# Adding the causal mask of a 16-head attention by VectorE in PSUM instead of by products on TensorE

## The chip, the cores and the metric

The kernel runs on one core of one Trainium2 chip. The metric is the device time of one execution in microseconds. The engines are TensorE (PE, with its weight loads shown as PEld), VectorE (DVE), ScalarE (ACT), GpSimd (POOL) and SyncE (SP), each with a queue of its own that it works through in order; they wait for one another on semaphores.

## The reference

The whole network has four layers of gated cross-attention and feed-forward on x of shape (4, 512, 128). The change lies in the feed-forward of the third layer, whose first half is a causal self-attention with 16 heads of width 64, run here for four batch elements of 512 tokens:

```python
ckv = x @ Wkva
kv_latent, k_rope = (ckv[:, :, :R], ckv[:, :, R:])
...
q = jnp.concatenate([q_nope, _rope(q_rope)], axis=-1)
k = jnp.concatenate([kv, _rope(k_rope)], axis=-1)
v = jnp.concatenate([kv, jnp.zeros_like(k_rope)], axis=-1)
att = jnp.einsum('bhqd,bhkd->bhqk', q, k) / jnp.sqrt(jnp.float32(D))
mask = jnp.tril(jnp.ones((t, t), dtype=bool))
att = jnp.where(mask, att, jnp.float32(-jnp.inf))
att = jax.nn.softmax(att, axis=-1)
y = jnp.einsum('bhqk,bhkd->bhqd', att, v)
```

The mixture of experts behind it, and the other layers, are not touched.

## The kernel before

The program is a sequence of blocks. `attention_2f(k, b, ...)` is the block of this attention, called once for each of the four batch elements. In it each engine has its own stream (`block.tensor`, `block.scalar`, `block.vector`, `block.gpsimd`). First come a normalisation and the projections with the rotation; then a loop over 32 units.

A unit u is one pair of heads (two of 16, side by side in the array's rows 0 to 63 and 64 to 127) and one tile of 128 queries. The four tiles of a pair come in the order 0, 1, 3, 2 (`tile_of`), and since attention is causal, tile t needs only the first 128(t+1) keys (`keys`): so the units of a pair have 128, 256, 512 and 384 keys. Here a unit is called by that number of keys; a pair (of heads) is four units. The last 128 keys of each unit are the diagonal tile, where the mask is needed: `causal` holds 0 on and below the diagonal and -3e38 above it.

What each engine does in one step of the loop, in its own order:

- PE (lines 2110 to 2122): `scores(u)`, lines 2058 to 2074, which needs the score banks that unit u-2 used, so it waits until both exps of u-2 are done (`s.ex`). It makes the products of both heads in two halves of the keys, then adds the mask to the diagonal tile by one product per head of a bf16 unit matrix with `causal_h`, a bf16 copy of `causal`, and signals `s.s`. Every eighth step `values(g)`, lines 2088 to 2099, the products with the latents for four heads. Then `turn(u-3, 0)` and `turn(u-3, 1)`, lines 2076 to 2086: transposes of the normalised rows of the two heads; each waits for POOL's normalised row (`s.pn`) and for the copy of the unit before out of its bank (`s.ca`, `s.cb`).
- DVE (lines 2203 to 2216): `copy_second(u-4)`, line 2201; `row_max(u)`, lines 2187 to 2191, the negated maximum of each head's row, read from PSUM; `reciprocals(u-1)`, line 2195.
- ACT (lines 2157 to 2172): `copy_first(u-3)`, line 2150; `exps(u)`, line 2142, one for each head, with the row's sum.
- POOL: `normalise(u)`, line 2026, each head's row times its reciprocal.

The score banks are four PSUM banks: two heads by two units in turn. After the loop come the last transposes, output products and the residual. The setup block makes `causal_h` once (line 589).

Of the kernel before, what the change touches and what calls it, by code (L numbers as in the profile page):

```python
# [16 lines left out]
BF16 = mybir.dt.bfloat16  # L17
I32 = mybir.dt.int32
ALU = mybir.AluOpType
# [3 lines left out]
P = 128  # L23
# [45 lines left out]
def flamingo_kernel(nc, a, at, early_at, out):  # L69
    with ExitStack() as ctx:  # L70
# [22 lines left out]
        def sb(name, shape, dt=FP32):  # L93
            return ctx.enter_context(nc.sbuf_tensor(name, shape, dt))
# [3 lines left out]
        def bank(i, n=1):  # L98
            return psum[:, 512 * i:512 * (i + n)]
# [40 lines left out]
        ident, causal, fold32 = resident("ident", P), resident("causal", P), resident("fold32", 32)  # L140
# [73 lines left out]
        qtt = part(region_b, 0, [P, PAIRS, S])  # L214
        turned_f = part(region_a, 0, [P, 4, T, S])
        krot = part(region_a, 4 * T * S, [P, S])
# [74 lines left out]
        latv = sb("latv", [P, T, 2 * LAT])  # L291
# [114 lines left out]
                       gsum=sb("gsum_f", [P, T]))  # L406
        back_ws = [set_m, back_w2, back_w3]
        ident_h = sb("ident_h", [P, P], BF16)
        causal_h = sb("causal_h", [P, P], BF16)
        fold_h = sb("fold_h", [96, 32], BF16)  # L410

        def over(ap, axis, shape):
            return ap.unsqueeze(axis).broadcast_to(shape)
# [85 lines left out]
        def setup(s):  # L499
# [77 lines left out]
            def vector(dve):  # L577
                link = chained(dve, s.dve)
                half = HD3 // 2
                yield 0  # L580
                nc.vector.memset(mka[:, :, :], 0.0)
                nc.vector.memset(latv[:, :, :], 0.0)
                nc.vector.memset(kctx[:, :, :], 0.0)
                nc.vector.memset(mkb[:, :, :], 0.0)
                nc.vector.memset(mqb[:, :, :], 0.0)
                nc.vector.memset(mqa[:, :, :], 0.0).then_inc(s.cleared, 1)
                dve.wait_ge(s.front_in, all_front)
                nc.vector.tensor_copy(ident_h[:, :], ident[:, :])
                nc.vector.tensor_copy(causal_h[:, :], causal[:, :])
                nc.vector.tensor_copy(fold_h[:, :], fold32[:, :])  # L590
                link(nc.vector.tensor_scalar(scale3[:, :], rs3[:, :], 1.0, None, ALU.add))
                yield 3
                for h in range(H3):
                    nc.vector.tensor_scalar(wk3a[:, h, :], wkv3[:, 0, :], scale3[:, 0:1], None, ALU.mult)
                    nc.vector.tensor_scalar(wk3b[:, h, 0:half], wkv3[:, 0, half:], scale3[:, 0:1], -1.0, ALU.mult, ALU.mult)
                    nc.vector.tensor_scalar(wk3b[:, h, half:], wkv3[:, 0, 0:half], scale3[:, 0:1], None, ALU.mult)
                    mm = nc.vector.tensor_scalar(wv3[:, h, :], wkv3[:, 1, :], scale3[:, 0:1], None, ALU.mult)
                mm.then_inc(s.wk3, 1)
                yield 7
                dve.wait_ge(s.exp2, 1)  # L600
                for _ in fp4_quantise(link, fw0[:, :, :], exp2_w[:, :], (big_r, big_r2), red[:, 0:4], red2[:, 0:4]):
                    pass
                nc.vector.tensor_tensor(big_r, big_r, over(red2[:, 0:4], 2, [P, 4, 32]), ALU.mult).then_inc(s.quantised, 1)
                yield 8
                nc.vector.tensor_scalar(wq3b[:, :, 0:half], wq3[:, :, half:], scale3[:, 0:1], -1.0, ALU.mult, ALU.mult)
                link(nc.vector.tensor_scalar(wq3b[:, :, half:], wq3[:, :, 0:half], scale3[:, 0:1], None, ALU.mult))
                link(nc.vector.tensor_scalar(wq3[:, :, :], wq3[:, :, :], scale3[:, 0:1], None, ALU.mult))
                yield 17
                dve.wait_ge(s.rest_in, all_rest)
                for r in range(2):  # L610
                    nc.vector.tensor_scalar(mka[:, r, 0:32], mkva[:, LAT:LAT + ROPE], wl1[:, 0:1], None, ALU.mult)
                    nc.vector.tensor_scalar(mka[:, r, 32:48], mkva[:, 0:LAT], wl1[:, 0:1], None, ALU.mult)
                    turn_k = mkb[:, r, 0:32].rearrange("p (i two) -> p i two", two=2)
                    pair_k = mkva[:, LAT:LAT + ROPE].rearrange("p (i two) -> p i two", two=2)
                    nc.vector.tensor_scalar(turn_k[:, :, 0], pair_k[:, :, 1], wl1[:, 0:1], -1.0, ALU.mult, ALU.mult)
                    nc.vector.tensor_scalar(turn_k[:, :, 1], pair_k[:, :, 0], wl1[:, 0:1], None, ALU.mult)
                dve.wait_ge(s.early_in, 16)
                dve.wait_ge(s.wl1_scaled, 1)
                nc.vector.tensor_scalar(mqa[:, :, 0:32], mq2[:, :, 32:64], rtmp[:, 0:1], None, ALU.mult)
                turn_q = mqb[:, :, 0:32].rearrange("p h (i two) -> p h i two", two=2)  # L620
                pair_q = mq2[:, :, 32:64].rearrange("p h (i two) -> p h i two", two=2)
                nc.vector.tensor_scalar(turn_q[:, :, :, 0], pair_q[:, :, :, 1], rtmp[:, 0:1], -1.0, ALU.mult, ALU.mult)
                nc.vector.tensor_scalar(turn_q[:, :, :, 1], pair_q[:, :, :, 0], rtmp[:, 0:1], None, ALU.mult)
                yield 21
                dve.wait_ge(s.be1_w2, E8)
                nc.vector.tensor_tensor(bias2[:, :], psum[:, 4 * 512:6 * 512], b2, ALU.add)
                for pair in range(4):
                    yield 22 + pair
                    dve.wait_ge(s.w2_mean, 1)
                    for e in (2 * pair, 2 * pair + 1):  # L630
                        cols = w2[:, FC * e:FC * (e + 1), 0:D]
                        mean = bank(6 + e // 4)[:, 128 * (e % 4):128 * (e % 4) + 128]
                        nc.vector.tensor_tensor(cols, cols, over(mean, 1, [P, FC, D]), ALU.subtract)
# [24 lines left out]
        NORM = ("stat", "mv", "rstd", "xn", "xt", "xnt")  # L658
# [923 lines left out]
        def attention_2(k, b, combined=None, last=None, also_load=None):  # L1582
# [75 lines left out]
            with nc.Block() as block:  # L1658
# [228 lines left out]
                def _(dve):  # L1887
# [43 lines left out]
                    for n in range(steps + 1):  # L1931
# [26 lines left out]
                                                   scalar=gate[:, 0, 2:3], in1=x[:, :, :], op0=ALU.mult, op1=ALU.add)  # L1958


        ATTENTION_2F = (*NORM, "pq", "cosm", "sinm", "rot", "lat", "latv", "s", "mx", "ex", "ri", "pn", "pn_last", "ta", "tb", "ca",
                        "cb", "o", "on", "y", "y1", *AHEAD)

        def attention_2f(k, b, x_next=None, copy_next=None, second_eps=None, early_loads=None):

            s = sems(k % 2, ATTENTION_2F)
# [9 lines left out]
            def keys(u):  # L1976
                return P * (tile_of(u) + 1)

            def s_bank(u, j):
                return bank(2 * (u % 2) + j)  # L1980
# [21 lines left out]
            with nc.Block() as block:  # L2002
# [33 lines left out]
                def _(pe):  # L2036
# [3 lines left out]
                    for n in range(PAIRS + 1):  # L2040
# [5 lines left out]
                        for j, w in enumerate((wa, wb)):  # L2046
                            mm = nc.tensor.matmul(bank(2 * (n % 2) + j), w[:, 2 * c:2 * c + 2, :].rearrange("p h k -> p (h k)"),
                                                  xnt[:, :], start=True, stop=True)
                        mm.then_inc(s.pq, 1)
                    for t in range(T):  # L2050
                        mm = nc.tensor.matmul(bank(6)[:, LAT * t:LAT * (t + 1)], xnt[:, P * t:P * (t + 1)],
                                              mka[:, 0, 32:48], start=True, stop=True)
# [5 lines left out]
                    def scores(u):  # L2058
                        p, t, n = u // T, tile_of(u), keys(u)
                        if u >= 2:  # L2060
                            pe.wait_ge(s.ex, 2 * (u - 1))
                        if t == 0:
                            pe.wait_ge(s.rot, p + 2)
                        pieces = 1 if t == 0 else 2
                        for h in range(pieces):
                            cols = slice(n // pieces * h, n // pieces * (h + 1))
                            for j in range(2):
                                lo = 64 * j
                                nc.tensor.matmul(s_bank(u, j)[:, cols], qtt[lo:lo + 64, p, P * t:P * (t + 1)],  # L2069
                                                 krot[lo:lo + 64, cols], start=(h == 0), stop=True, skip_group_check=True)  # L2070
                        for j in range(2):
                            mm = nc.tensor.matmul(s_bank(u, j)[:, n - P:n], ident_h[:, :], causal_h[:, :],  # L2072
                                                  start=False, stop=True, skip_group_check=True)
                        mm.then_inc(s.s, 1)

                    def turn(u, j):
# [99 lines left out]
                def _(dve):  # L2176
# [9 lines left out]

                    def row_max(u):
                        dve.wait_ge(s.s, u + 1)
                        for j in range(2):
                            nc.vector.tensor_reduce(nmax[:, 2 * u + j:2 * u + j + 1], s_bank(u, j)[:, 0:keys(u)], AX.X, ALU.max,  # L2190
                                                    negate=True).then_inc(s.mx, 1)
# [1035 lines left out]
        for b in range(B):  # L3227
            k = next_block()
# [121 lines left out]
```

## Time and profile before

| | |
|---|---|
| median of the timed executions | 1777.54 us |
| profiled execution | 1780.08 us, its span 1778.3 us |
| busy over the span | PE 1569.0, DVE 1173.9, ACT 773.4, POOL 848.4 us |
| mean granted TensorE clock | 0.948 of 2.4 GHz |
| loops of the changed stage, four times | within 528 to 596, 773 to 841, 1017 to 1086, 1486 to 1555 us |

The span is the time from the first to the last instruction on the core; the time of an execution includes what lies around it. A busy time counts the instructions of an engine; PE's products are pipelined and their ends are modelled. In a timeline a row is one instruction or a merged run of equal ones (xN), with the start in us from the span's start and the time from the start of the first to the end of the last; the bracket names how long the engine had been idle before and what released it. "issue" means that it waited for nothing that the profile shows.

### The profile page before, as it was taken

The page shows a single profiled execution, that of the slowest core. Times are in us where ns is not written, and L with a number is a line of the kernel's source. Part 1 is how long each engine was busy: PE and PEld are TensorE (multiplying, and loading weights), DVE is VectorE, ACT ScalarE, POOL GpSimd, SP SyncE. Part 2 cuts the span into 40 slices and gives each one's busy share as a digit, 9 for nine tenths or more (in the row PEclk, how much of TensorE's full clock was granted, in tenths as well). Part 3 has the DMA queues.
Part 4 walks back from the last instruction along what each step waited for, and adds up shares of the span by engine and source line. Part 5 has one row for each costly group of instructions (what it writes and reads, how often), then busy time and mean ns, then how long its engine had stood idle before and what let it go on. Part 6 is the DMA issues. An engine that isn't in the chain of part 4 may idle for free. (4 is left out here: it accounts for less than half of the span.)

```text
span 1778.3 us, 30950 instructions
## 1 busy us (share of the span) xinstructions
PE 1569.0 (88%) x10175; PEld 1075.3 (60%) x10175; DVE 1173.9 (66%) x3120; ACT 773.4 (43%) x1974; POOL 848.4 (48%) x1075
## 2 busy tenths in 40 slices
PE   5655599899999999999899997958999999989899
PEld 4545376647756557756477565435656775668666
DVE  6867677857847567566578475476847756645657
ACT  2321244436617456447366174313225653744422
POOL 2551734538747367566287464010645656600072
PEclk7876799999999999999999997979999999999999
DMA  9200022100000310000000001004420000145363
GB/s 306 80 13 1 31 95 78 43 8 12 1 1 1 125 53 6 1 2 1 2 12 1 1 2 48 0 1 151 145 69 1 1 1 19 48 167 140 107 167 112
DMA packets 76539, 91.33 MB, mean 51 GB/s; under 512 B 10536, under 2 KB 57256, under 8 KB 75072
## 3 DMA queue, kind: packets, MB, share of 16 engines
q1 hardware_dynamic: 71264, 78.86, 14.0%
q0 software_dynamic: 5120, 10.50, 2.1%
q8 instruction: 86, 1.41, 0.3%
q14 instruction: 69, 0.57, 0.1%
HBM read 69.14 MB, written 27.66 MB: 54 GB/s over the span
## 5 line engine op out<-in xcount | busy, mean ns | idle before, releaser
L1677 POOL TENSOR_TENSOR rows<-rows,rinv 128x512 f32<-128x512 f32 x192 | 198.5, 1062 | 117.5 <-DVE rinv L1917 117.5
L1841 ACT ACTIVATE rows<-psum,nmax 128x512 f32<-128x512 f32 x192 | 130.0, 683 | 122.1 <-DVE nmax L1910 122.0
L2026 POOL TENSOR_TENSOR rows<-rows,rinv 128x128 f32<-128x128 f32 (+2 forms) x192 | 127.1, 684 | 76.8 <-DVE rinv L2195 76.8
L1909 DVE TENSOR_REDUCE lg<-psum 128x2 f32<-128x1024 f32 x128 | 155.7, 1217 | 3.2
L1921 DVE COPY turned<-psum 128x512 f32<-128x512 f32 x128 | 88.2, 689 | 80.4 <-PE psum L1737 79.4
L2190 DVE TENSOR_REDUCE nmax<-psum 128x1 f32<-128x128 f32 (+3 forms) x256 | 113.7, 486 | 41.7 <-PE psum L2072 40.7
L1725 PE MATMUL psum<-region_a,region_b 64*128 64x256 f32 x1024 | 130.6, 391 | 6.0 <-ACT rows L1841 2.9
L1758 PE MATMUL psum<-turned,region_a 128*64 128x256 f32 x1024 | 124.6, 385 | 0.4
L2069 PE MATMUL psum<-region_a,region_b 64*128 64x128 f32 (+2 forms) x896 | 105.8, 349 | 10.5 <-ACT rows L2142 4.6
L1725 PEld LDWEIGHTS psum<-region_a,region_b 64*128 64x128 f32 x1024 | 92.8, 186 | 28.9 <-ACT rows L1841 7.7
L1737 PEld LDWEIGHTS psum<-weights,rows 128*128 128x128 f32 x768 | 82.0, 140 | 44.9 <-issue 23.0
L1737 PE MATMUL psum<-weights,rows 128*128 128x128 f32 x768 | 103.3, 279 | 3.9 <-ACT turned L1850 2.4
L2142 ACT ACTIVATE rows<-psum,nmax 128x128 f32<-128x128 f32 (+2 forms) x192 | 96.2, 510 | 11.2 <-DVE nmax L2190 11.2
L2584 ACT ACTIVATE region_b<-psum 128x512 f32<-128x512 f32 x66 | 39.4, 598 | 139.1 <-PE psum L2546 139.1
L1758 PEld LDWEIGHTS psum<-turned,region_a 128*64 128x64 f32 x1024 | 68.6, 136 | 47.1 <-issue 19.6
L1850 ACT ACTIVATE turned<-psum 128x512 f32<-128x512 f32 x128 | 76.7, 599 | 46.0 <-PE psum L1737 46.0
L2069 PEld LDWEIGHTS psum<-region_a,region_b 64*128 64x128 f32 x896 | 69.4, 187 | 34.6 <-ACT rows L2142 11.9
L2558 PEld LDWEIGHTS psum<-region_c,region_b 128*128 128x128 f32 x512 | 66.1, 192 | 27.9 <-issue 22.7
L2084 PE MATMUL psum<-weights,rows 128*128 128x128 f32 x448 | 76.2, 280 | 6.6 <-DVE region_a L2201 1.7
L1703 PE MATMUL psum<-kvt,weights 128*128 128x512 f32 x128 | 65.6, 642 | 11.1 <-PEq L765 7.5
L2850 POOL DMA_INDIRECT sorted<-turned,small_f x48 | 49.1, 1023 | 51.1 <-DVE small_f L2784 36.7
L1689 POOL TENSOR_TENSOR ysb<-ysb,nmax 128x128 f32<-128x128 f32 x64 | 25.8, 403 | 94.6 <-DVE nmax L1910 93.7
(866 smaller groups left out, 3922.8 us busy)
## 6 DMA issues: line engine op xcount, KB each, us to landing
pt<-gates SPq DMA_DIRECT2D x64, 128.0 KB
ysb<-gates SPq DMA_DIRECT2D x64, 128.0 KB
weights<-sorted SPq DMA_DIRECT2D x28, 256.0 KB, 3.3
made<-weights SPq DMA_DIRECT2D x28, 256.0 KB, 2.4
sorted<-sorted SPq DMA_DIRECT2D x4, 1536.0 KB, 13.6
sorted<-kctx SPq DMA_DIRECT2D x2, 1536.0 KB
region_b<-sorted SPq DMA_DIRECT2D x12, 256.0 KB, 3.6
made<-rows SPq DMA_DIRECT2D x12, 256.0 KB, 2.4
```

The lines of the kernel that those rows point to most:

```text
L1677: nc.gpsimd.tensor_tensor(row(u, j), row(u, j), rinv[:, 2 * u + j:2 * u + j + 1].broadcast_to([P, S]), ALU.mult).then_inc(s.pn, 1)
L1725: mm = nc.tensor.matmul(s_bank(u, j)[:, 256 * half:256 * (half + 1)], qtt[lo:lo + 64, p, P * t:P * (t + 1)], ktt[lo:lo + 64, p, 256 * half ...
L1737: mm = nc.tensor.transpose(turn_bank(place(n, i))[:, P * k:P * (k + 1)], row(u, j)[:, P * k:P * (k + 1)], ident[:, :])
L1758: nc.tensor.matmul(bank(7)[lo:lo + HD2, 256 * half:256 * (half + 1)], vtok[:, k, P * p + lo:P * p + lo + HD2], turned2[:, 2 * half + j, k, :],
L1841: nc.scalar.activation(row(u, j), s_bank(u, j), ACT.Exp, bias=nmax[:, 2 * u + j:2 * u + j + 1], accum_out=sum_column(u // T, u % T, j)).th ...
L1850: nc.scalar.activation(turned_to(n, i), turn_bank(place(n, i)).rearrange("p (k q) -> p k q", q=P), ACT.Copy).then_inc(s.ca, 1)
L1909: link(nc.vector.tensor_reduce(maxima(u // T)[:, both(u), 0], both_scores(u), AX.X, ALU.max, negate=True))
L1921: nc.vector.tensor_copy(turned_to(n, i), turn_bank(place(n, i)).rearrange("p (k q) -> p k q", q=P)).then_inc(s.cb, 1)
L2026: nc.gpsimd.tensor_tensor(head, head, rinv[:, 2 * u + j:2 * u + j + 1].broadcast_to([P, keys(u)]), ALU.mult).then_inc(s.pn, 1)
L2069: nc.tensor.matmul(s_bank(u, j)[:, cols], qtt[lo:lo + 64, p, P * t:P * (t + 1)], krot[lo:lo + 64, cols], start=(h == 0), stop=True, skip_g ...
L2142: nc.scalar.activation(rows_of(u)[:, j, 0:keys(u)], s_bank(u, j)[:, 0:keys(u)], ACT.Exp, bias=nmax[:, 2 * u + j:2 * u + j + 1], accum_out= ...
L2190: nc.vector.tensor_reduce(nmax[:, 2 * u + j:2 * u + j + 1], s_bank(u, j)[:, 0:keys(u)], AX.X, ALU.max, negate=True).then_inc(s.mx, 1)
```

## The change

The bf16 copy of the mask and the two mask products of a unit go. The scores' last product now signals `s.s`. On VectorE `row_max` first adds `causal`, the fp32 table in SBUF, to the diagonal tile of both heads in one instruction, in place in PSUM, signals the new semaphore `s.masked`, waits for it, and then takes the two maxima as before.

```diff
+        ATTENTION_2F = (*NORM, "pq", "cosm", "sinm", "rot", "lat", "latv", "s", "masked", "mx", "ex", "ri", "pn", "pn_last", "ta", "tb", "ca",
...
-        causal_h = sb("causal_h", [P, P], BF16)
...
-                nc.vector.tensor_copy(causal_h[:, :], causal[:, :])
...
                             for j in range(2):
                                 lo = 64 * j
-                                nc.tensor.matmul(s_bank(u, j)[:, cols], qtt[lo:lo + 64, p, P * t:P * (t + 1)],
-                                                 krot[lo:lo + 64, cols], start=(h == 0), stop=True, skip_group_check=True)
-                        for j in range(2):
-                            mm = nc.tensor.matmul(s_bank(u, j)[:, n - P:n], ident_h[:, :], causal_h[:, :],
-                                                  start=False, stop=True, skip_group_check=True)
+                                mm = nc.tensor.matmul(s_bank(u, j)[:, cols], qtt[lo:lo + 64, p, P * t:P * (t + 1)],
+                                                      krot[lo:lo + 64, cols], start=(h == 0), stop=True, skip_group_check=True)
                         mm.then_inc(s.s, 1)
...
                     def row_max(u):
                         dve.wait_ge(s.s, u + 1)
+                        own_tile = bank(2 * (u % 2), 2).rearrange("p (j k) -> p j k", j=2)[:, :, keys(u) - P:keys(u)]
+                        nc.vector.tensor_tensor(own_tile, own_tile, over(causal[:, :], 1, [P, 2, P]), ALU.add).then_inc(s.masked, 1)
+                        dve.wait_ge(s.masked, u + 1)
                         for j in range(2):
```

## Rows read from the trace of the kernel before

**Rows 1.** Busy time by window, first of four such loops: us, busy by engine, clock, DMA
```profile
528.00:596.00 68.00, 63.60 (x578) 43.68 (x577) 48.36 (x144) 49.06 (x165) 47.54 (x68) 1.00 0.01 2
```

**Rows 2.** One line of the code: the mask's products, count, ns min/median/max, first and last start
```profile
L2072 PE MATMUL psum<-causal_h,ident_h x256: 219/229/314, 530.9 to 1550.6; 128*128 128x128 bf16 x128
```

**Rows 3.** Timeline, one plain pair: start us, us, engine, line, instruction [idle before <-releaser]
```profile
555.04 1.14 PE L2069 MATMUL psum<-region_a,region_b 64*128 64x256 f32 x8
...
556.10 0.11 PEld L2072 LDWEIGHTS psum<-causal_h,ident_h 128*128 128x128 bf16 x2 [0.33 <-issue]
...
556.11 0.29 PE L2072 MATMUL psum<-causal_h,ident_h 128*128 128x128 bf16 x2
556.17 0.64 PEld L2084 LDWEIGHTS psum<-weights,turned 128*128 128x128 f32 x6
...
556.43 1.29 DVE L2190 TENSOR_REDUCE nmax<-psum 128x1 f32<-128x512 f32 x2 [0.59 <-PE psum L2072]
...
556.99 0.92 PE L2069 MATMUL psum<-region_a,region_b 64*128 64x192 f32 x8
557.24 0.69 ACT L2142 ACTIVATE rows<-psum,nmax 128x512 f32<-128x512 f32 x1
557.64 0.15 DVE L2195 RECIPROCAL rinv<-psum_of 128x2 f32<-128x2 f32 x1
557.71 0.54 DVE L2201 COPY region_a<-psum 128x384 f32<-128x384 f32 x1
...
557.92 0.68 ACT L2142 ACTIVATE rows<-psum,nmax 128x512 f32<-128x512 f32 x1
...
558.16 1.02 DVE L2190 TENSOR_REDUCE nmax<-psum 128x1 f32<-128x384 f32 x2
...
558.74 0.30 PEld L2069 LDWEIGHTS psum<-region_a,region_b 64*128 64x128 f32 x4 [0.24 <-ACT rows L2142]
...
559.10 0.15 DVE L2195 RECIPROCAL rinv<-psum_of 128x2 f32<-128x2 f32 x1
...
559.34 2.04 POOL L2026 TENSOR_TENSOR rows<-rows,rinv 128x512 f32<-128x512 f32 x2 [0.28 <-DVE rinv L2195]
559.41 0.57 ACT L2142 ACTIVATE turned<-psum,nmax 128x384 f32<-128x384 f32 x1
...
560.12 0.52 PEld L2069 LDWEIGHTS psum<-region_a,region_b 64*128 64x128 f32 x8 [0.36 <-ACT turned L2142]
...
561.42 0.42 PEld L2084 LDWEIGHTS psum<-weights,rows 128*128 128x128 f32 x4 [0.17 <-POOL rows L2026]
...
562.01 0.73 PEld L2069 LDWEIGHTS psum<-region_a,region_b 64*128 64x128 f32 x8 [0.17 <-issue]
```

**Rows 4.** Timeline, TensorE in the next pair, which holds the `values` products
```profile
565.71 0.49 PE L2069 MATMUL psum<-region_a,region_b 64*128 64x128 f32 x4
...
566.35 2.36 PE L2096 MATMUL psum<-region_a,latv 128*32 128x512 f32 x32
...
569.23 0.71 PE L2069 MATMUL psum<-region_a,region_b 64*128 64x128 f32 x8
...
570.97 1.14 PE L2069 MATMUL psum<-region_a,region_b 64*128 64x256 f32 x8
```

**Rows 5.** VectorE's instructions by line and form: count, busy us, mean ns, idle before
```profile
L2190 DVE TENSOR_REDUCE nmax<-psum 128x1 f32<-128x384 f32 x64 | 32.6, 552 | 0.4 <-PE psum L2072 0.4
...
L1055 DVE TENSOR_TENSOR pt<-psum,weights 128x256 f32<-128x256 f32 x4 | 1.7, 425 | 11.9 <-PE psum L904 11.9
...
L2184 DVE TENSOR_TENSOR region_b<-psum,weights 128x512 f32<-128x512 f32 x32 | 22.2, 692 | 13.7 <-PE psum L2047 13.7
...
L3000 DVE TENSOR_TENSOR region_b<-region_b,small_f 128x512 f32<-128x512 f32 x28 | 19.4, 692 | 1.0
```

**Rows 6.** Timeline of VectorE in the setup, where the second waits for the first's semaphore
```profile
35.04 0.29 DVE L427 TENSOR_TENSOR region_c<-weights,small_f 128x128 f32<-128x128 f32 x1
35.36 0.23 DVE L428 TENSOR_SCALAR region_c<-region_c 128x128 f32<-128x128 f32 x1
```

More of the change, by code:

```diff
@@ L1958, in _ @@
                                                    scalar=gate[:, 0, 2:3], in1=x[:, :, :], op0=ALU.mult, op1=ALU.add)
-        ATTENTION_2F = (*NORM, "pq", "cosm", "sinm", "rot", "lat", "latv", "s", "mx", "ex", "ri", "pn", "pn_last", "ta", "tb", "ca",
+        ATTENTION_2F = (*NORM, "pq", "cosm", "sinm", "rot", "lat", "latv", "s", "masked", "mx", "ex", "ri", "pn", "pn_last", "ta", "tb", "ca",
                         "cb", "o", "on", "y", "y1", *AHEAD)
```

## The prediction

> **What bounds the kernel now.** I read the busy time by window first, because the change touches one stage that runs four times. In the loop of the first batch (68 us) PE is busy 63.60 us, VectorE (DVE) 48.36, ACT 49.06, POOL 47.54, at granted clock 1.00, the 2.4 GHz level; the other three loops (windows 773 to 841, 1017 to 1086, 1486 to 1555) differ by under 2 us an engine [rows 1]. PE seems to bind, but no engine is far behind. So I went to the timeline of one head pair, which is four units in the order 128, 256, 512, 384 keys. From the scores of the 512 unit at 555.04 to those of the next at 562.01 a pair takes 6.97 us [rows 3]. Every second pair from the fourth on also holds the `values` products: the scores of the 256 unit then start 3.52 us after those of the 128 unit (565.71 to 569.23) instead of 1.38, and such a pair takes 8.96, from 562.01 to 570.97 [rows 3, 4]. In a plain pair PE isn't saturated; it stands still at three places. The scores of the 128 unit wait 0.24 for an exp of ACT, those of the 256 unit 0.36 for another, and a transpose at 561.42 waits 0.17 for POOL [rows 3]. These are the ends of chains scores, row maximum (DVE), exp (ACT), reciprocal (DVE), normalise (POOL). The DVE steps of a chain therefore cost time in plain pairs although DVE is free over a quarter of the time.
>
> **What the change removes.** Two bf16 products a unit, 256 in all, 229 ns each by the median, with overlap [rows 2]. In PE's own order they are worth far less: the mask's weight load is at 556.10 and the transposes' at 556.17, so 0.07 us a unit [rows 3]. The semaphore to DVE gains more: the last score product ends at 555.04 + 1.14 = 556.18, the mask at 556.11 + 0.29 = 556.40 [rows 3], so DVE can start 0.22 earlier. The bf16 copy of the causal table in the setup goes too, one instruction of a few tenths of a microsecond at most once in the run; I count nothing.
>
> **What it adds.** One tensor_tensor on 128x256 elements a unit, 128 in all, PSUM in, PSUM out, with the table from SBUF, and a wait for its own end before the first maximum. The nearest row has the same size and sources but writes SBUF: 425 ns [rows 5]. DVE's instructions overlap when none waits: two reduces of 552 ns [rows 5] take 1.02 together [rows 3], so the second starts 0.08 before the first ends, and an unwaited add would cost 0.42 - 0.08 = 0.34 of the queue. Where one waits for the other's semaphore, the next starts at 35.36 after 35.04 + 0.29 = 35.33, so 0.03 behind its end [rows 6]. The add with its wait thus costs 0.42 + 0.03 = 0.45. No row shows DVE writing PSUM. From below I take 0.34 (no price for the wait), from above the 692 ns of 128x512 [rows 5], as if reading and writing the same bank took a pass each, 0.72 with the wait. I use 0.45: 128x512 takes 692 ns whether one source is in PSUM or both are in SBUF [rows 5], and I assume that writing makes as little difference. Queued behind the waiting add are both maxima, the reciprocal of the unit before, and the copy of the second head; ACT's exps, POOL's normalise and PE's second transposes wait for these.
>
> The Trainium skill (VectorE: DVE Perf Modes, "The DRAIN you can't avoid") says that a semaphore after each of a chain of DVE operations costs nothing more, since the pipe is flushed anyway. By it the add would cost what an unwaited one does; rows 3 and 6 show 0.34 against 0.45. That is the third rival below.
>
> **The walk through a plain pair**, in us from the scores of the 512 unit, before in brackets. All durations and spacings are those of [rows 3].
> Unit 512: scores end 1.14; DVE adds from 1.17 and starts the maxima at 1.62 [556.43, so 1.39]. The two take 1.29 together and overlap by 0.08, so each is 0.69 long and the second starts 0.60 or 0.61 after the first; they end at 2.31 and 2.91. ACT starts the first exp at 2.34 [2.20], the second 0.68 later at 3.02 [2.88], and the 128 unit's scores start 0.82 behind that, at 3.84 [3.70].
> Unit 384: PE reaches its scores at 1.87 [1.94] and ends them 0.93 later at 2.80. DVE isn't free: after the maxima it has the reciprocal (from 1.62 + 1.21 = 2.83, 0.07) and the copy of the second head (0.45), to 3.35. The add starts there, the maxima at 3.80 [558.16, so 3.12]. Here the early semaphore of the scores brings nothing and two adds have come into DVE's queue: 1.39 + 1.73 = 3.12 has become 1.62 + 1.73 + 0.45. The first maximum ends 4.35, exps start 4.38 and 4.95 [second: 4.37], and the 256 unit's scores come 0.71 behind, at 5.66 [5.08].
> POOL: the reciprocal of the 512 unit starts behind the maxima of 384, at 3.80 + 0.94 = 4.74 [559.10, so 4.06]. POOL starts 0.24 after it, at 4.98 [4.30], needs 2.04, to 7.02; the last four transposes load at 7.06 [561.42, so 6.38], and the next 512 scores start 0.59 behind, at 7.65 [6.97].
> So a plain pair costs 7.65 - 6.97 = 0.68 more. The 128 unit's maxima start at about 5.45 and no longer matter for 7.65; DVE reaches the 256 unit's maxima by 6.85 and ends its queue of the pair near 7.5, so it carries no debt into the next pair.
>
> **A pair with values.** The 128 unit's scores at 3.84, the 256's 3.52 - 0.07 = 3.45 later at 7.29, and the next 512 scores 1.74 - 0.07 behind at 8.96: as before. Here the 2.36 us of products [rows 4] hide the adds and the shorter PE order pays for the longer chain. If that cover were gone, such a pair would cost what a plain one does, 0.68.
>
> **Sum.** Per batch 8 pairs, three with `values` in the loop (g = 0, 1, 2 at steps 12, 20, 28), five plain: 5 x 0.68 = 3.4 us; four batches 13.6 us. The norm, projection and output parts around the loop don't change, and nothing else runs beside the stage, so the delay goes through whole. The profiled execution would go from 1780.08 (span 1778.3) to 1793.7; its own time stands 2.54 above the median 1777.54, to which I add the same 13.6: 1791.1. I predict 1791.
>
> **Rivals.**
> 1. The add is dearer (a price of PSUM in place, or a longer semaphore path). Each 0.01 of it comes twice into a plain pair: 0.02 x 20 = 0.4 us in the run. Slower by over 1% begins 4.2 us above my value, that is at an add of 0.45 + 0.105 = 0.555 with its wait. At the upper bound 0.72 a plain pair costs 0.68 + 0.54 = 1.22, 24.4 us, and the value pairs, whose chain to the 128 unit is 0.27 longer, another 12 x 0.27 = 3.2: 27.6, so 1805. For it: no row writes PSUM from DVE. Against it: all DVE rows follow size alone.
> 2. DVE's idle quarter takes the adds and only PE's relief remains: 128 x 0.07 = 9.0 us less, 1768.6. For it: PE is the busiest in [rows 1], and the adds come to 4 x 0.45 = 1.8 us a pair, 32 x 0.45 = 14.4 a batch against the 68 - 48.36 = 19.6 that DVE is free. Against it: the three stalls in [rows 3] hang on DVE, so the path isn't PE's order alone.
> 3. The wait costs nothing: the add is 0.34. Then a plain pair costs 0.68 - 0.22 = 0.46, 9.2 us, so 1787. For it: the skill's rule named above; against it the gap in [rows 6] beside the overlap in [rows 3].
> That the change does nothing is excluded: 256 PE instructions go and 128 DVE ones come.
>
> **How the numbers follow.** Forecast (12 to 18 us more): 0.40. Rival 1 above 1795: 0.32. Rival 3 and what lies between it and the forecast, 5 to 12 us more: 0.15. Rival 2 in full or in part (9 less to 5 more): 0.12. Rest 0.01. About 1% is what a measurement of this kernel can tell from no change, 1759.8 to 1795.3: faster 0.02, same 0.65, slower 0.33. The range runs from 1779, which leaves out most of rival 2, to 1806, just over the upper bound of the add's price.
>
> **What the profile after would show.** The add near 0.42 us, the first maximum 0.03 behind its end; steps between scores of a plain pair near 1.87, 1.97, 1.82 and 1.99 instead of 1.94, 1.76, 1.38 and 1.89; value pairs of 8.96 still; the waits of PE for ACT and POOL grown by about half a microsecond each in plain pairs; DVE busy about 128 x 0.42 = 54 us more; granted clock still 1.00 in the loops. Rival 2 would show plain pairs under 6.97. I would be wrong if the add took over 0.5 us, if PE's transposes didn't move up when the mask goes, or if ACT's order hid the later maxima.

## The result, and the profile after

| | before | after |
|---|---|---|
| median | 1777.49 us (1777.35 to 1793.15) | 1823.93 us (1813.91 to 1824.84) |
| profiled execution, span | 1780.08, 1778.3 us | 1823.12, 1821.3 us |
| mean granted TensorE clock | 0.948 | 0.932 |
| DVE busy | 1173.9 us | 1222.3 us |

The changed kernel is slower: ratio 1.0208, 95% interval 1.0156 to 1.0259, which leaves open whether by more than 2%. The forecast was 1791, with 1806 as the upper end.

First the time by stage. I cut each span at the first projection product and at the last residual of each of the four attention blocks; a block between those points is called a stage here. These are the busy times by window of the kernel after: us, then the busy time of PE, PEld, DVE, ACT and POOL, granted clock, DMA share, GB/s. The second, third, fourth and sixth rows are the stages, the first and the fifth are code that the change leaves as it was.

```profile
0.00:517.60 517.60, 411.41 (x2490) 301.17 (x2490) 368.91 (x1168) 198.00 (x457) 248.30 (x323) 0.88 0.18 57
517.60:614.80 97.20, 85.29 (x592) 54.73 (x592) 72.60 (x196) 50.96 (x169) 56.08 (x74) 0.93 0.00 1
...
771.10:867.10 96.00, 84.03 (x592) 53.62 (x592) 72.47 (x196) 50.90 (x169) 56.06 (x74) 0.95 0.01 1
...
1023.40:1119.20 95.80, 83.70 (x588) 53.18 (x588) 70.45 (x184) 49.93 (x166) 54.82 (x72) 0.95 0.01 1
1119.20:1508.50 389.30, 343.98 (x1830) 221.44 (x1830) 240.14 (x616) 137.48 (x295) 145.29 (x184) 0.92 0.15 48
1508.50:1604.40 95.90, 83.66 (x588) 53.16 (x588) 70.31 (x184) 50.03 (x166) 54.83 (x72) 0.95 0.11 39
```

The same cuts of the kernel before; the second and the fourth row are the first and the last stage (the two between them took 88.9 and 88.7 us at clock 1.00).

```profile
0.00:513.40 513.40, 406.94 (x2490) 299.12 (x2490) 368.06 (x1169) 197.69 (x457) 248.28 (x323) 0.88 0.18 58
513.40:602.10 88.70, 82.62 (x656) 52.19 (x656) 60.58 (x164) 50.63 (x169) 56.10 (x74) 1.00 0.00 1
...
1092.50:1473.00 380.50, 336.12 (x1830) 217.10 (x1830) 240.26 (x616) 137.63 (x295) 145.33 (x184) 0.93 0.15 49
1473.00:1563.00 90.00, 84.01 (x652) 52.62 (x652) 58.51 (x152) 49.86 (x166) 54.86 (x72) 0.98 0.12 43
```

A stage took 88.7 us and takes 97.2; the four sum to 384.9 against 356.3, so 28.6 us more. The other 14.4 of the 43.0 between the spans lie in unchanged code: the first part is 4.2 longer, the part between the third and the fourth stage 8.8, the rest 1.4. And the clock of the stages, 1.00, 1.00, 1.00 and 0.98 before ([rows 1] is the loop of the first), is 0.93 to 0.95 now. A stretch's time at the lower level (1.2 GHz) is twice its length times one minus its mean clock: 97.2 x 0.07 x 2 = 13.6 us in the first stage. Since these clocks are rounded to 0.01, the sums of four stages below are added up from windows of 4 us: 44.4 us in the kernel after, against 3.4 before, all of it in the fourth stage.

Now a plain pair at full clock, which answers to [rows 3]: the timeline of the kernel after, start us, us, engine, line, instruction. L2067 are the scores, L2185 the add, L2188 the maxima, L2137 the exps.

```profile
563.04 1.14 PE L2067 MATMUL psum<-region_a,region_b 64*128 64x256 f32 x8
...
564.23 0.43 DVE L2185 TENSOR_TENSOR psum<-psum,weights 128x256 f32<-128x256 f32 x1 [0.21 <-PE psum L2067]
...
564.69 1.29 DVE L2188 TENSOR_REDUCE nmax<-psum 128x1 f32<-128x512 f32 x2
...
564.91 0.92 PE L2067 MATMUL psum<-region_a,region_b 64*128 64x192 f32 x8
565.50 0.69 ACT L2137 ACTIVATE rows<-psum,nmax 128x512 f32<-128x512 f32 x1 [0.32 <-DVE nmax L2188]
...
566.18 0.68 ACT L2137 ACTIVATE rows<-psum,nmax 128x512 f32<-128x512 f32 x1
566.43 0.42 DVE L2185 TENSOR_TENSOR psum<-psum,weights 128x256 f32<-128x256 f32 x1
...
566.65 0.30 PE L2079 MATMUL psum<-weights,rows 128*128 128x128 f32 x1 [0.56 <-DVE region_a L2199]
...
566.88 1.02 DVE L2188 TENSOR_REDUCE nmax<-psum 128x1 f32<-128x384 f32 x2
567.00 0.30 PEld L2067 LDWEIGHTS psum<-region_a,region_b 64*128 64x128 f32 x4 [0.24 <-ACT rows L2137]
...
567.82 0.15 DVE L2193 RECIPROCAL rinv<-psum_of 128x2 f32<-128x2 f32 x1
...
568.05 2.04 POOL L2024 TENSOR_TENSOR rows<-rows,rinv 128x512 f32<-128x512 f32 x2 [0.74 <-DVE rinv L2193]
...
568.31 0.41 PE L2079 MATMUL psum<-weights,rows 128*128 128x128 f32 x2 [0.45 <-DVE region_a L2199]
...
568.84 0.52 PEld L2067 LDWEIGHTS psum<-region_a,region_b 64*128 64x128 f32 x8 [0.36 <-ACT turned L2137]
...
570.14 0.42 PEld L2079 LDWEIGHTS psum<-weights,rows 128*128 128x128 f32 x4 [0.24 <-POOL rows L2024]
...
570.73 0.73 PEld L2067 LDWEIGHTS psum<-region_a,region_b 64*128 64x128 f32 x8 [0.17 <-issue]
```

From 563.04 to 570.73 the pair takes 7.69 us, where 7.65 was forecast and 6.97 was before. The pair with `values` behind it ends at 579.65, 8.92 us later (8.96 forecast, 8.96 before). So the walk held to 0.04 us a pair, and what it left out of the stages is TensorE's clock.

### The profile page after: what moved, and what is told of

It is laid out like the page before. It is cut to its first block and busy times, and to the rows that moved or that the text cites. A ratio compares the mean times of both kernels' runs of the same rounds, so it can differ in the third digit from the quotient of the medians.

```text
span 1821.3 us, 30565 instructions
## 1 busy us (share of the span) xinstructions
PE 1590.1 (87%) x9919; PEld 1089.8 (60%) x9919; DVE 1222.3 (67%) x3247; ACT 774.3 (43%) x1974; POOL 848.2 (47%) x1075
## 3 DMA queue, kind: packets, MB, share of 16 engines
q8 instruction: 84, 1.38, 0.3%
## 5 line engine op out<-in xcount | busy, mean ns | idle before, releaser
L2067 PE MATMUL psum<-region_a,region_b 64*128 64x128 f32 (+2 forms) x896 | 111.1, 367 | 14.9 <-ACT rows L2137 9.3
L2188 DVE TENSOR_REDUCE nmax<-psum 128x1 f32<-128x128 f32 (+3 forms) x256 | 113.7, 486 | 4.4
L2079 PE MATMUL psum<-weights,rows 128*128 128x128 f32 x448 | 89.7, 315 | 25.2 <-DVE region_a L2199 14.8
L1723 PEld LDWEIGHTS psum<-region_a,region_b 64*128 64x128 f32 x1024 | 93.0, 187 | 28.7 <-ACT rows L1839 7.7
L1735 PEld LDWEIGHTS psum<-weights,rows 128*128 128x128 f32 x768 | 82.0, 141 | 44.8 <-issue 24.1
L1735 PE MATMUL psum<-weights,rows 128*128 128x128 f32 x768 | 103.3, 279 | 3.8 <-ACT turned L1848 2.4
L2137 ACT ACTIVATE rows<-psum,nmax 128x128 f32<-128x128 f32 (+2 forms) x192 | 95.9, 507 | 23.9 <-DVE nmax L2188 23.9
L2067 PEld LDWEIGHTS psum<-region_a,region_b 64*128 64x128 f32 x896 | 74.7, 201 | 40.9 <-ACT rows L2137 17.4
L2079 PEld LDWEIGHTS psum<-weights,rows 128*128 128x128 f32 x448 | 56.6, 156 | 52.6 <-issue 43.6
```

Source lines behind the costliest of these rows:

```text
L1723: mm = nc.tensor.matmul(s_bank(u, j)[:, 256 * half:256 * (half + 1)], qtt[lo:lo + 64, p, P * t:P * (t + 1)], ktt[lo:lo + 64, p, 256 * half ...
L1735: mm = nc.tensor.transpose(turn_bank(place(n, i))[:, P * k:P * (k + 1)], row(u, j)[:, P * k:P * (k + 1)], ident[:, :])
L2067: mm = nc.tensor.matmul(s_bank(u, j)[:, cols], qtt[lo:lo + 64, p, P * t:P * (t + 1)], krot[lo:lo + 64, cols], start=(h == 0), stop=True, s ...
L2079: mm = nc.tensor.transpose(bank(4 + j)[:, P * k:P * (k + 1)], rows_of(u)[:, j, P * k:P * (k + 1)], ident[:, :])
L2137: nc.scalar.activation(rows_of(u)[:, j, 0:keys(u)], s_bank(u, j)[:, 0:keys(u)], ACT.Exp, bias=nmax[:, 2 * u + j:2 * u + j + 1], accum_out= ...
```

## The experiments

Stage sums below are the sum of the four stages of one profiled execution: 356.3 us before, 384.9 after.

**The removal alone.** The scores' last product signals, and nobody adds a mask.

```diff
-                        for j in range(2):
-                            mm = nc.tensor.matmul(s_bank(u, j)[:, n - P:n], ident_h[:, :], causal_h[:, :],
-                                                  start=False, stop=True, skip_group_check=True)
                         mm.then_inc(s.s, 1)
```

> Only the removal: the mask's 256 products go and nothing replaces them (the causal mask is left out of the result). Theory (the walk is right and the rest of the 46 us is TensorE's clock, which falls where TensorE waits for VectorE): no wait is added, so the clock of the four loops stays at 0.98 to 1.00 and the walk's relief shows, 7 us less than before, 1770. Rival (the mask products themselves kept the clock up, their removal is what costs): the loops fall to about 0.94 to 0.95 as in the changed kernel and the time is 1785 or more.

Measured: ratio 0.9932 (0.9898 to 0.9966), the stages 87.5, 87.1, 87.6 and 87.7 us at clock 0.98, 0.98, 0.98 and 0.96, in sum 349.9. The relief is there, 6.4 us. The clock stands between the theory (0.98 to 1.00) and the rival (0.94 to 0.95): with fewer products, 17.1 us of the stages ran at the lower level instead of 3.4. Losing the products does weigh on the clock, but not as much as the whole change. It isn't a pure test of fewer products, though: at the loop's start TensorE also waits longer for ACT's exps without them, 0.78 and 1.21 us where it had been 0.36 and 0.97.

**The addition alone.** VectorE adds, and TensorE keeps its products, of zeros.

```diff
+                nc.vector.memset(causal_h[:, :], 0.0)
...
+                        for j in range(2):
+                            mm = nc.tensor.matmul(s_bank(u, j)[:, n - P:n], ident_h[:, :], causal_h[:, :],
+                                                  start=False, stop=True, skip_group_check=True)
                         mm.then_inc(s.s, 1)
```

> Only the addition: VectorE adds the mask as in the changed kernel, and TensorE keeps its 256 products, of a table of zeros, so its order and its amount of products are those of before. The walk with the mask's end as signal gives 0.9 us more a plain pair and 0.2 more a pair with values: 22 us more at full clock, 1799. Theory (the waits for VectorE bring the clock down): some further 10 to 30 us, 1810 to 1830, with the loops' clock below 0.97. Rival (the removed products kept the clock up): clock 0.98 to 1.00 in the loops and 1799.

Measured: 1817.7 us, ratio 1.0169 (1.0111 to 1.0226), stages 95.9, 96.6, 96.0 and 99.2 at clock 0.98, 0.98, 0.98 and 0.93, in sum 387.7, with 23.9 us at the lower level. The time lies in the theory's range. Three of the four stages stand at 0.98, nearer to the rival's clock than to the theory's, and the last at 0.93: the waits too weigh on the clock, again by less than waits and lost products together. How much time that cost, the run with both and the fill below bears on. TensorE's weight loads of the scores of 512 keys in this kernel:

```profile
566.93 0.73 PEld L2069 LDWEIGHTS psum<-region_a,region_b 64*128 64x128 f32 x8 [0.17 <-issue]
...
576.36 0.73 PEld L2069 LDWEIGHTS psum<-region_a,region_b 64*128 64x128 f32 x8 [0.17 <-issue]
...
584.25 0.73 PEld L2069 LDWEIGHTS psum<-region_a,region_b 64*128 64x128 f32 x8 [0.17 <-issue]
```

The second to the third is a plain pair, 7.89 us, where the walk gave 6.97 + 0.9; the first to the second is a pair with `values`, 9.43, where it gave 8.96 + 0.2. So 12 x 0.27 = 3.2 us of the 31.4 are a term of this walk that I had too small.

**The changed kernel with TensorE kept busy.** Two fp32 products of 128x512 at the loop's start and a few small bf16 ones in every pair, all into a bank that holds nothing at that time.

```diff
+                    def fill(u):
+                        if u in (2, 4):
+                            nc.tensor.matmul(bank(7), mqa[:, 0:2, :].rearrange("p h k -> p (h k)"), xnt[:, :], start=True, stop=True)
...
                     def scores(u):
                         p, t, n = u // T, tile_of(u), keys(u)
+                        fill(u)
...
                                 turn(step - LAG, 0)
+                                if tile_of(step - LAG) < 3:
+                                    fill_small(step - LAG, 6 if tile_of(step - LAG) < 2 else 2)
                                 turn(step - LAG, 1)
```

`fill_small` issues that many products `nc.tensor.matmul(free[:, 0:P], ident_h[:, :], ident_h[:, :], start=True, stop=True)`; from step 20 on it waits for `s.on` first.

> The changed kernel with TensorE kept busy while it waits: two fp32 products of 128x512 into a free bank ahead of the scores of units 2 and 4, and 2 to 6 bf16 products of 128x128 between the transposes of the two heads in each unit of 128, 256 or 384 keys. Nothing else changes. Theory (clock): the loops' clock returns to 0.98 to 1.00 and the time to what the walk gave, 1791, within 5 us (the fill may cost a few). Rival (the excess is stalls of another kind): it stays at 1813 or above.

Measured: 1802.83 us (1800.82 to 1805.71), ratio 1.0081 (1.0055 to 1.0108). The four stages are 93.5, 93.5, 93.4 and 93.5 us, all at clock 1.00, in sum 373.9. More work for TensorE made the stages 11.0 us shorter. The time is 1803, between the theory (1791 within 5) and the rival (1813 or above). Of the 12 us over 1791, some 4 were the fill's own price in pairs with `values` (9.26 where the changed kernel has 8.92, 12 times), and 8 lie in the unchanged parts, 1430.0 in this profile against 1422.0.

**Only the fill at the loop's start.** The same without `fill_small`.

> The changed kernel with only the two fp32 products ahead of the scores of units 2 and 4, none in the plain pairs. If the clock falls because of the sparse start of each loop alone, the four stages take 93 us each at clock 1.00, as with both fills. If the waits within the plain pairs count too, a drop stays in the loops and after them, the clock of the stages is 0.96 to 0.98 and they take 94 to 96 us.

Measured: 1809.58 us, ratio 1.0118 (1.0083 to 1.0154), stages 93.6, 95.3, 93.6 and 94.9 at clock 0.98, 0.96, 0.98 and 0.96, in sum 377.4. At the lower level ran 20.5 us of the stages instead of 44.4, so about half of it hangs on the sparse start of the loop and the rest on the waits of the pairs and of the loop's end. It is the second of the two forecasts, with two stages a little under its 94 us.

**A fill that lies in the waits alone.**

```diff
-                                if tile_of(step - LAG) < 3:
-                                    fill_small(step - LAG, 6 if tile_of(step - LAG) < 2 else 2)
+                                if tile_of(step - LAG) < 2 and not (step > 8 and step % 8 == 4):
+                                    fill_small(step - LAG, 6)
```

> The changed kernel with a fill that lies only in TensorE's waits: the two fp32 products ahead of the scores of units 2 and 4, and six bf16 products between the transposes of the two heads in the units of 128 and 256 keys, but none in the step that holds values and none in the unit of 384 keys, where the fuller fill lengthened the pairs with values from 8.96 to 9.26. Theory: at clock 1.00 the four stages cost the walk's 13.6 us over the 356.3 of before, 370, against 374 with the fuller fill and 384.6 without any. Rival (fills themselves cost nothing and the walk is 4 us short): 374 again. Rival (with less fill the clock drops): 375 or more with the clock below 1.00.

The busy times by window of two of its stages:

```profile
517.80:610.10 92.30, 86.17 (x674) 54.68 (x674) 72.41 (x196) 50.97 (x169) 56.16 (x74) 1.00 0.00 1
...
766.50:858.80 92.30, 85.92 (x674) 54.67 (x674) 72.47 (x196) 50.91 (x169) 56.13 (x74) 1.00 0.01 1
```

Each of the four stages takes 92.3 us at clock 1.00, in sum 369.2: 12.9 over before, where the walk gave 13.6. The scores of 512 keys in this kernel:

```profile
560.94 1.14 PE L2080 MATMUL psum<-region_a,region_b 64*128 64x256 f32 x8
...
568.62 1.14 PE L2080 MATMUL psum<-region_a,region_b 64*128 64x256 f32 x8
...
577.55 1.13 PE L2080 MATMUL psum<-region_a,region_b 64*128 64x256 f32 x8
```

A plain pair is 568.62 - 560.94 = 7.68 us, one with `values` 8.93. The clock's share of the changed kernel's stages is then 384.9 - 369.2 = 15.7 us, or more by what the fill itself costs them. The kernel before has a small share of its own: its fourth stage, with 3.4 us at the lower level, took 1.3 us more than its third. With both at full clock the stages differ by 369.2 - 355.0 = 14.2 us, near the 13.6 of the walk, and the clock makes the other 14.4 of the 28.6. The whole kernel took 1798.11 us at the median of 10 (1793.57 to 1811.74), ratio 1.0094 (1.0056 to 1.0131) to a median of 1780.8 of the kernel before on that chip. It doesn't beat the kernel before.

**Both, filled.** VectorE's add, the products of zeros, and the full fill.

> VectorE's add and TensorE's 256 products of zeros, with the full fill of the first filled kernel. Without fill the stages took 387.7, 31.4 over before, where the walk gave 22. Theory (the rest is the clock): at clock 1.00 they come to 356.3 + 22 and some 4 for the fill, 380 to 384. Rival (the walk underrates the add where the mask's end gives the signal): 387 or more at clock 1.00.

Measured in one profiled execution: stages of 96.3, 96.4, 96.2 and 96.3 us at clock 1.00, in sum 385.2, so 1 us over the theory's 380 to 384, 2 under the rival's 387, and 2.5 under the unfilled 387.7. It settles little: how the 385.2 split between the fill and the add it doesn't show. But it doesn't bear out the 10 to 30 us that I had given to the clock in the kernel with both: there 23.9 us at the lower level cost 2.5 us and what the fill itself costs, which no run measures there. The share of 15.7 us is shown for the changed kernel alone.

**One column instead of 128.** The add and its wait stay, on one column of each head.

```diff
-                        own_tile = bank(2 * (u % 2), 2).rearrange("p (j k) -> p j k", j=2)[:, :, keys(u) - P:keys(u)]
-                        nc.vector.tensor_tensor(own_tile, own_tile, over(causal[:, :], 1, [P, 2, P]), ALU.add).then_inc(s.masked, 1)
+                        own_tile = bank(2 * (u % 2), 2).rearrange("p (j k) -> p j k", j=2)[:, :, keys(u) - 1:keys(u)]
+                        nc.vector.tensor_tensor(own_tile, own_tile, over(causal[:, P - 1:P], 1, [P, 2, 1]), ALU.add).then_inc(s.masked, 1)
```

> The changed kernel with the add on one column of each head instead of 128 (the causal mask is left out but for one column). VectorE's instruction and its wait stay, at some 0.15 to 0.18 us instead of 0.45. By the walk the pairs are as long as before, within 1 us over the run; the clock should be that of the kernel without any mask (0.96 to 0.98), where TensorE has as few products and waits as little: stages 350 to 358 us in all. If the number of VectorE's instructions and the wait were what costs, whatever the length, the stages stay above 370.

The add in this kernel: count, ns min/median/max, first and last start.

```profile
L2185 DVE TENSOR_TENSOR psum<-psum,weights x128: 148/168/169, 537.2 to 1567.7; 128x2 f32<-128x2 f32 x128
```

Ratio 1.001 (0.998 to 1.0039), stages 90.1, 88.6, 90.1 and 89.6 at clock 0.98, 1.00, 0.98 and 0.98, in sum 358.4. That is just above the 350 to 358 that I gave, and 8.5 us over the kernel without any mask (349.9): so much the extra instruction and its wait cost, with less time at the lower level (10.2 us against 17.1). The other 26.5 of the changed kernel's 384.9 come with the length of the add, 429 ns instead of 168, in a chain that TensorE waits for. They are no pure price of the chain: a plain pair is 7.16 us here (scores of 512 keys at 562.55 and 569.71) and one with `values` 8.66, so the pairs account for 20 x 0.53 + 12 x 0.26 = 13.7 us. The other 12.8 I put down to the clock, with 10.2 us at the lower level here and 44.4 there; no run separates them for this pair of kernels.

**The mask ahead of the scores, in the kernel before.** The scores are then added onto the mask (`start=False` in all of them), and their last product signals.

```diff
+                        for j in range(2):
+                            nc.tensor.matmul(s_bank(u, j)[:, n - P:n], ident_h[:, :], causal_h[:, :],
+                                             start=True, stop=False, skip_group_check=True)
                         for h in range(pieces):
...
-                        for j in range(2):
-                            mm = nc.tensor.matmul(s_bank(u, j)[:, n - P:n], ident_h[:, :], causal_h[:, :],
-                                                  start=False, stop=True, skip_group_check=True)
```

> The kernel before with the two mask products of a unit ahead of its scores instead of behind them, so that the signal to VectorE comes 0.15 us earlier at the same amount of products. By the walk 0.14 us less in a plain pair, 3 us less in all: 1774.5. If TensorE's own order alone binds, no difference: 1777.5. The clock of the loops as before.

Ratio 0.9984 (0.9944 to 1.0024), stages 356.9: no difference. TensorE's weight loads in a plain pair, L2066 the mask, L2072 the scores:

```profile
555.11 0.64 PEld L2084 LDWEIGHTS psum<-weights,turned 128*128 128x128 f32 x6 [0.33 <-issue]
...
555.71 0.21 PEld L2066 LDWEIGHTS psum<-causal_h,ident_h 128*128 128x128 bf16 x2
...
556.02 0.63 PEld L2072 LDWEIGHTS psum<-region_a,region_b 64*128 64x128 f32 x8
...
557.57 0.11 PEld L2066 LDWEIGHTS psum<-causal_h,ident_h 128*128 128x128 bf16 x2 [0.28 <-ACT rows L2142]
557.79 0.30 PEld L2072 LDWEIGHTS psum<-region_a,region_b 64*128 64x128 f32 x4
```

From the mask's weight load to the scores' it is 0.31 us, while behind the scores the mask had taken 0.07 from the transposes [rows 3]. Part of the 0.31 was there before, between transposes and scores: from the load of these six transposes to that of the scores it is 556.02 - 555.11 = 0.91 us with the mask in between, and was 0.81 without. In the units of 128 and 256 keys the mask now stands between ACT's exp and the scores: it loads at 557.57, as soon as the exp is done, and the scores follow 0.22 later. In this pair the scores of 512 keys come at 554.04 and again at 560.96, so it takes 6.92 us against 6.97, a gain of 0.05 where the walk gave 0.14, and the stages don't show even that.

**The same two kernels once more.**

> The changed kernel again, on another chip: does the time outside its four attention stages, whose code is the same as before and which took 14 us more, repeat? Theory (that part is TensorE's clock wandering between executions and not the change): the stages take 95 to 98 us each again, while the rest differs from 1436 by several microseconds. Rival (the new kernel puts the later parts into a worse clock every time): the rest is 1436 within 2 us again.

> The kernel before, profiled a second time. In its 25 timed executions it fell into two groups, near 1778 and near 1792. Theory: the four stages are 88 to 90 us each as in the first profile, and where it is 1792, the 14 us lie in the parts that the change leaves alone. Rival: they lie in the four stages (then 92 or more each).

The stages of the changed kernel came to 384.3 (384.9 the first time), those of the kernel before to 356.3 (356.3). The unchanged parts came to 1430.8 (1436.4) and 1435.1 (1422.0). Three windows of the kernel before in its second profile, where the execution took 1793.25 us:

```profile
0.00:519.20 519.20, 414.69 (x2489) 304.60 (x2489) 369.09 (x1169) 198.09 (x457) 248.23 (x323) 0.89 0.18 57
519.20:607.90 88.70, 82.67 (x656) 52.26 (x656) 60.59 (x164) 50.58 (x169) 56.06 (x74) 1.00 0.00 1
...
1100.00:1486.00 386.00, 341.75 (x1831) 221.56 (x1831) 240.27 (x616) 137.38 (x295) 145.30 (x184) 0.92 0.15 48
```

The first and the third are the parts that had looked longer in the changed kernel; here they are 5.8 and 5.5 us longer than in the first profile of the same kernel, and the stage is the same 88.7. So the 14.4 us of the first comparison are no effect of the change that I can show: over all profiles these parts summed to 1422.0 to 1439.1, with no order by kernel that I can see. The changed kernel's median in this second measurement was 1821.61, ratio 1.0189 (1.0151 to 1.0227).

## Why the prediction was wrong

**What held.** The add's price: 429 ns, in place in PSUM, where I took 425.

```profile
L2185 DVE TENSOR_TENSOR psum<-psum,weights x128: 411/429/433, 535.3 to 1590.5; 128x256 f32<-128x256 f32 x128
```

Its wait: the maxima start at 564.69 behind 564.23 + 0.43, 0.03 as in [rows 6], so the add with its wait is 0.46 (0.45 taken). Rival 3, by which the wait is free, falls: 0.46 stands against 0.34. Rival 1, the dearer add, falls too: the time passed its upper bound of 1805 with the add at the lower price. The walk: scores of 384 keys at 1.87 (1.87), second add at 3.39 (3.35), the 512 unit's reciprocal at 4.78 (4.74), the last transposes at 7.10 (7.06), the next pair at 7.69 (7.65). One spacing was too small: the first exp comes 0.12 behind its maximum where I took 0.03, though [rows 3] already had the 0.12 (maximum to 556.43 + 0.69 = 557.12, exp at 557.24). So the scores of the 128 unit are at 3.96 instead of 3.84 and those of the 256 unit at 5.80 instead of 5.66. That this did no harm is luck: neither ends the pair. The sum of 13.6 us was 12.9 once the clock was held, or 14.2 against the kernel before at full clock too.

Two of the signs I gave were off. The waits of TensorE for ACT ahead of the scores are 0.24 and 0.36 as before, and that for POOL is 0.24 instead of 0.17; what grew are its waits for VectorE's copies out of the transposes' banks, to 0.56 and 0.45 us. A pair before has one of them, which I had not counted among its three stalls:

```profile
558.39 0.30 PE L2084 MATMUL psum<-weights,rows 128*128 128x128 f32 x1 [0.15 <-DVE region_a L2201]
```

And VectorE's busy time rose by 48.4 us, not by 54.

**What failed.** The sentence "nothing else runs beside the stage, so the delay goes through whole", and the line "granted clock still 1.00 in the loops". I had put the clock down as something to look at and gave it neither a rival nor a chance, though it was the one term that grows when TensorE waits more. The kernel after in windows of 4 us from the first scores on:

```profile
534.00:538.00 4.00, 2.13 (x21) 1.47 (x21) 2.72 (x9) 1.98 (x9) 2.03 (x4) 1.00 0.00 0
538.00:542.00 4.00, 2.55 (x20) 1.70 (x18) 3.80 (x11) 2.78 (x10) 1.97 (x4) 0.91 0.00 0
542.00:546.00 4.00, 4.00 (x26) 3.04 (x24) 2.79 (x9) 2.54 (x12) 3.79 (x6) 0.67 0.00 0
546.00:550.00 4.00, 3.26 (x24) 2.04 (x22) 3.70 (x10) 2.67 (x9) 1.18 (x2) 1.00 0.00 0
550.00:554.00 4.00, 3.56 (x22) 2.82 (x24) 3.15 (x11) 3.12 (x14) 3.94 (x6) 0.69 0.02 4
```

and the same stretch of the kernel before:

```profile
530.00:534.00 4.00, 3.12 (x28) 2.15 (x30) 1.89 (x7) 1.98 (x9) 2.08 (x4) 1.00 0.00 0
534.00:538.00 4.00, 2.89 (x30) 1.96 (x28) 3.38 (x11) 3.43 (x13) 2.71 (x4) 1.00 0.00 0
538.00:542.00 4.00, 4.00 (x38) 3.04 (x37) 3.02 (x8) 2.96 (x11) 2.81 (x6) 1.00 0.01 4
```

In the first 8 us TensorE was busy for 2.13 + 2.55 us where it had been for 3.12 + 2.89, and the clock falls to 1.2 GHz near 541 and again near 551. (A window at 2.4 GHz shows 1.00, one at 1.2 GHz 0.50; 0.67 is a mix.) What lies in it, TensorE's rows of the kernel after:

```profile
536.92 2.13 PE L2067 MATMUL psum<-region_a,region_b 64*128 64x256 f32 x16 [1.24 <-ACT rows L2137]
...
540.79 0.49 PE L2067 MATMUL psum<-region_a,region_b 64*128 64x128 f32 x4 [1.38 <-ACT rows L2137]
...
543.47 1.66 PE L2079 MATMUL psum<-weights,rows 128*128 128x128 f32 x8
```

and of the kernel before:

```profile
532.46 1.13 PE L2069 MATMUL psum<-region_a,region_b 64*128 64x256 f32 x8 [0.36 <-ACT rows L2142]
...
536.07 0.49 PE L2069 MATMUL psum<-region_a,region_b 64*128 64x128 f32 x4 [0.97 <-ACT rows L2142]
...
538.14 1.04 PE L2084 MATMUL psum<-weights,rows 128*128 128x128 f32 x8
```

The loop's start is sparse because no transposes are due yet. TensorE waited 0.36 and 0.97 us there for ACT's exps; now it waits 1.24 and 1.38, since each exp comes later by the add. Then the eight transposes take 1.66 us where they took 1.04. The same drop comes in each of the four stages, and once more behind the loop. By an estimate part of the lost time hides in waits: 44.4 us at half the clock are 22.2 us of lost work, and holding the clock gave 15.7. Neither cause explains the time at the lower level alone, and together they nearly add up: it was 3.4 us of the stages before, 13.7 more without the products, 20.5 more with the add alone, 41.0 more in the changed kernel, and none with TensorE kept busy.

The waits don't decide it by themselves. The kernel before fell in its fourth stage too, near the same place of the loop, in both of its profiles, after the wait of 0.36 us alone (the second was 0.24 there):

```profile
1490.00:1494.00 4.00, 3.47 (x26) 2.20 (x26) 1.39 (x6) 1.83 (x8) 2.03 (x3) 0.80 0.00 0
```

So the loop's start was near a fall before the change, and the change made it fall in every stage. What exactly sets the moment these runs don't show.

The Trainium skill (TensorE: Matmul & The Clock Gate, "HAM oscillation — how this bites in real kernels") says that waits between bursts of products bring TensorE's clock down. The trace agrees in direction, with the waits of 1.24 and 1.38 us above; the waits for transfers in its example are longer than any of these. I had passed over that rule because all stages but the last stood at 1.00, and a clock at 1.00 doesn't show how near it is to falling; the last, at 0.98, did show it.

**The rest of the miss.** The medians differ by 46.4 us: 28.6 lie in the stages, 12.9 by the walk and 15.7 by the clock as measured against the filled kernel, and the other 17.8 outside them. Some of these are chance: of the first four executions of the kernel before three took 1777.4 to 1777.5 us, near the lowest it ever showed. Over all 55, on several chips, its median is 1786.9, over all 8 of the changed kernel 1823.5, which is 36.6 apart. The last 8 us of that I can't place: the unchanged parts of two profiles of each kernel overlap (1422.0 and 1435.1, 1436.4 and 1430.8), so no effect of the change on them is shown, nor excluded. Against the median 1777.49 of the first measurement even the right stage sum gives 1806, at the end of my range, not 1824. Rival 2, TensorE's own order as the bound, was wrong in direction but its term was near in size: the removal alone gave 6.4 us where the 0.07 us a unit made 9.0.

## What to carry to other kernels

Before work is moved off TensorE onto an engine that it waits for, look where TensorE is already sparse (a loop's start and end, where the pipeline is not full) and price a fall of its clock there: here it cost as much as the move itself. When a stage gets slower than its walk says, put the granted clock beside it in narrow windows before looking for another stall, and prove it by giving TensorE idle work: it made these stages 15.7 us shorter. And compare stages between profiles, not whole times alone, where unchanged parts wander by as much as the effect.

## What the runs showed of the hardware that I had not expected

- In the first stage of the changed kernel, with waits of 1.24 and 1.38 us near the start of the loop, the clock fell from 2.4 to 1.2 GHz, and it fell there in the other three too; in that of the kernel before, with waits of 0.36 and 0.97 in the same place, it held, but in the fourth it fell all the same, for 3.4 us.
- Six bf16 products of 128x128, put into each of two waits a pair, with two larger ones at the loop's start, held the clock at 1.00 through all four stages and cost the plain pairs nothing (7.68 against 7.69 us).
- VectorE adds in place in PSUM at the price of another place, 429 ns for 128x256 against 425 into SBUF.
- From the load of two full-array bf16 products to that of products on 64 rows it is 0.31 us, to that of full-array transposes 0.07; TensorE's order between transposes and scores grew by 0.10 with the mask in it.
- The same program, the same code: between two profiles of the kernel before the unchanged first part took 513.4 and 519.2 us and the part before the last stage 380.5 and 386.0. The 55 timed executions of that kernel lie between 1775.6 and 1793.4 us; the 25 on one chip fall into two groups, 1777 to 1781 and 1791 to 1793.
